# Sending each token's row to its expert slots in DRAM by indirect writes, in place of a one-hot token table and gathers

## The chip, the core and the metric

The kernel runs on one core of one Trainium2 chip. The metric is the device time of one execution in microseconds (us), smaller is better; a comparison takes the median of several runs. One further execution is recorded by the hardware profiler, and every duration below comes from that record.

## What is computed

Cross-attention with a gate, then a mixture of experts with a gate. There are 32 x 128 = 4096 tokens of 256 values, 8 experts, two experts for each token, and room for `cap` = 1024 tokens in each expert. Cut to what matters here:

```python
x = x + tanh(g_xattn) * xattn(layernorm(x), ctx)           # 16 heads of 64
xf = layernorm(x).reshape(4096, 256)
topv, topi = top_k(softmax(xf @ gate_w.T), 2)
gates = topv / topv.sum(-1)
# loc[t, j]: how many tokens chose this expert before this one;
# all first choices count before all second choices
valid = loc < 1024
flat_idx = where(valid, topi * 1024 + loc, 0)
disp = zeros(8 * 1024, 256).at[flat_idx].add(xf * valid)    # dispatch
h = relu(disp_e @ fc1_e.T + fc1_b);  eo = h @ fc2_e + fc2_b # for each expert e
out = (eo[flat_idx] * (gates * valid)).sum(over the two choices)
x = x + tanh(g_ffn) * out
```

## The kernel before, in words

The program has two blocks, one after the other, with a barrier of all five engines between them. Each engine runs a stream of its own that is written out by hand; semaphores order the engines, and no scheduler moves anything. Matrix products with weights are made of three (or five) products of split operands, a high and a low part of each.

**Attention** (`attention`). The tokens go in 8 groups `g` of 512 (`GB` = 4 batches of 128 tokens). A group has 8 steps `j` (`NP`), one for each pair of heads. In a step TensorE computes a queries tile (L591 to L593), a keys tile (L599 to L603), a values tile (L471 to L475), the scores (L514), transposes the probabilities of the step before (L488) and weighs the values of the step before that (L501). VectorE finds the maxima of the scores (L917), normalises (L947), evicts the transposes (L884) and the values (L909). ScalarE takes the exponentials (L722). In step 7 TensorE also transposes the next group's rows (L479, jobs FA and FB), ScalarE writes their high part and VectorE their low part `xT_l` (`low`, L760), which the next group's first query needs. TensorE's results go through two PSUM banks in turn (`take_bank`): a job waits until the job two before it has been evicted.

The routing of group g-1 is spread over the steps of group g: output projection and residual in step 1 (`residual`), second layer norm in step 2 (`normalise`, L779, tile `xn2`), gate logits in step 3 (`route_masks`), ranks in step 4 (`route_counts`), slots in step 5 (`route_slots`), which ends with `hl`, the slot of each token and choice cut into a high and a low part (L865). From `hl` GpSimd and VectorE build one-hot rows (`onehots`, L227, L228, L230). In step 7 TensorE multiplies them in the jobs T0 and T1 (L560), which puts token number and gate at each slot's place, and VectorE adds that to `table` (L936). GpSimd's order in a group is: bias onto the residual rows (L399), two `rstd`, the split of the next context (`split_cv`), the one-hots, then `copy_ck` (L338), whose result `ck` the next group's first keys tile (L599) waits for. SyncE loads x and context of the next group, stores x1 to the output (L285) and the normalised rows to `xn2_dram` (L287). After the last group a tail (`finish`) runs the same routing steps with nothing beside them. `keep_warm` (L111) fills waits of TensorE with products that nobody reads.

**Experts** (`experts`). Each expert has 2 groups `n` of 512 slots, 16 in all. GpSimd gathers the rows of a group from `xn2_dram` by four indirect DMAs (`gather`, L1117), with columns of `index` from the table; TensorE transposes them (`transpose_rows`, L1185), multiplies with fc1 (L1199 to L1201) and fc2 (L1213 to L1215); VectorE adds the bias (L1302), ScalarE scales by the gate (L1258), and GpSimd adds the rows to the output by four indirect DMAs with addition (`scatter`, L1129). GpSimd also makes the low parts of the next expert's weights (L1139, L1141). The transposes of the next group stand in the middle of a group, between fc1 and fc2.

Of the kernel before, what the change touches and what calls it, by code (L numbers as in the profile page):

```python
# [5 lines left out]
P = 128  # L6
# [17 lines left out]
NHI = E * CAP // P  # L24
EH = CAP // P
PAD = 1
# [31 lines left out]
MISC_PREV = {1: ["O0", "O1"], 2: ["XA", "XB"], 3: ["LG"], 4: ["PR"], 7: ["T0", "T1"]}  # L58
# [15 lines left out]
def gated_block(nc, x, ctxT, g_x, g_f, wq, wk, wv, wo, bo, gateT, fc1T, fc1b, fc2, fc2b, out):  # L74
    f32 = mybir.dt.float32

    xn2_dram = nc.dram_tensor("xn2_rows", [N + PAD, D], f32, kind="Internal").ap()
# [3 lines left out]
    xn2_v = xn2_dram[0:N, :].rearrange("(b p) d -> p b d", p=P)  # L81

    with ExitStack() as keep:
# [4 lines left out]
        table = keep.enter_context(nc.sbuf_tensor("table", [P, 2, 2, NHI], f32))  # L88
# [10 lines left out]
        keep2 = keep.enter_context(nc.sbuf_tensor("keep2", [P, E, EH], f32))  # L99
        shared = (keep2, table, running, tanh_g, ident, w1_raw, w2_raw, w1_split, w2_split)  # L100

        with ExitStack() as ctx:
            attention(nc, ctx, sem, x_v, out_v, xn2_v, xn2_dram, ctxT, g_x, g_f, wq, wk, wv, wo, bo, gateT, fc1T, fc2, shared)
        with ExitStack() as ctx:
            experts(nc, ctx, sem, out_rows, xn2_dram, fc1T, fc1b, fc2, fc2b, shared)
# [13 lines left out]
def attention(nc, ctx, sem, x_v, out_v, xn2_v, xn2_dram, ctxT, g_x, g_f, wq, wk, wv, wo, bo, gateT, fc1T, fc2, shared):  # L119
# [7 lines left out]
    keep2, table, running, tanh_g, ident, w1_raw, w2_raw, w1_split, w2_split = shared  # L127
# [19 lines left out]
    onehot_lo = work[:, 1024:2048].rearrange("p (s k) -> p s k", s=8)  # L147
    rows = sb("rows", [P, 4, GB, D])
    xn, xr, x1, xn2 = (rows[:, n] for n in range(4))

    flat_rows = rows.rearrange("p a b d -> p a (b d)")
    wv_raw, wk_raw = [work[:, 0:INNER], flat_rows[:, 1]], [flat_rows[:, 2], flat_rows[:, 3]]
    hi_vals = rows[:, 3].rearrange("p b (two c) -> p (b two) c", two=2)
# [6 lines left out]
    zrow = sb("zrow", [PAD, D])  # L160
# [9 lines left out]
    gates, gdiff, gexp, gden = sb("gates", [P, 2, GB]), sb("gdiff", [P, GB]), sb("gexp", [P, GB]), sb("gden", [P, GB])  # L170
    place, loc, late, slot = sb("place", [P, 2, GB, E]), sb("loc", [P, 2, GB]), sb("late", [P, 2, GB]), sb("slot", [P, 2, GB])
    ranks = sb("ranks", [P, 2 * 2 * GB * E])
    sloti, hl_i = sb("sloti", [P, 2, GB], i32), sb("hl_i", [P, 2, 2, GB], i32)
    hl = sb("hl", [P, 2, 2, GB])
# [4 lines left out]
    def ps(name):  # L179
# [8 lines left out]
        s_consts, s_wo_in, s_c_in, s_x_in, s_xr_in, s_small_in, s_zeros_out, s_w_hi,  # L188
        s_w_lo, s_tanh, s_bias_o, s_zrow, s_q_ready, s_k_ready, s_v_ready, s_s_ready, s_pt_ready,
        s_av_ready, s_o_ready, s_xt_ready, s_lg_ready, s_pr_ready, s_tb_ready, s_f_ready, s_at_hi,  # L190
        s_f_hi, s_q_done, s_k_done, s_v_done, s_pt_done0, s_pt_done1, s_at_split, s_f_split, s_negmax,
        s_exp, s_p_ready, s_o_done, s_xa_done, s_xb_done, s_lg_done, s_pr_done, s_tb_done, s_stats1,
        s_rstd1, s_xn_ready, s_stats2, s_rstd2, s_xn2_ready, s_mask_ready, s_gdiff, s_gexp,
        s_slot_ready, s_onehot0, s_onehot1, s_onehot_last, s_token, s_cv_ready, s_ck_ready, s_xr_ready, s_x1_out, s_xn2_out, s_w_rest,
        s_dve_self, s_pool_self, s_dve_gate, s_pool_gate, s_e0_in, s_c0_hi, s_e0_hi, s_e0_lo,
    ) = (sem("a_" + name) for name in (
        "consts", "wo_in", "c_in", "x_in", "xr_in", "small_in", "zeros_out", "w_hi",
        "w_lo", "tanh", "bias_o", "zrow", "q_ready", "k_ready", "v_ready", "s_ready", "pt_ready",
        "av_ready", "o_ready", "xt_ready", "lg_ready", "pr_ready", "tb_ready", "f_ready", "at_hi",
        "f_hi", "q_done", "k_done", "v_done", "pt_done0", "pt_done1", "at_split", "f_split", "negmax",  # L200
        "exp", "p_ready", "o_done", "xa_done", "xb_done", "lg_done", "pr_done", "tb_done", "stats1",
        "rstd1", "xn_ready", "stats2", "rstd2", "xn2_ready", "mask_ready", "gdiff", "gexp",
        "slot_ready", "onehot0", "onehot1", "onehot_last", "token", "cv_ready", "ck_ready", "xr_ready", "x1_out", "xn2_out", "w_rest",
# [6 lines left out]
    def done(job, g):  # L210

        kind, j = job
        return {
            "Q": (s_q_done, 8 * g + j + 1), "K": (s_k_done, 8 * g + j + 1), "V": (s_v_done, 8 * g + j + V_AHEAD + 1),
            "O0": (s_o_done, 2 * g - 1), "O1": (s_o_done, 2 * g), "XA": (s_xa_done, g), "XB": (s_xb_done, g),
            "LG": (s_lg_done, g), "PR": (s_pr_done, g), "T0": (s_tb_done, 2 * g + 1), "T1": (s_tb_done, 2 * g + 2),
            "FA": (s_f_split, 2 * g + 3), "FB": (s_f_split, 2 * g + 4),
        }[kind]
# [3 lines left out]

    def onehots(engine, j, batches=range(GB)):

        for b in batches:
            n = j * GB + b
            engine.tensor_scalar(onehot_lo[:, n, :], iota[:, :], hl[:, 1, j, b:b + 1], None, ALU.is_equal)  # L227
            engine.tensor_scalar(hi_vals[:, n, 0:NHI], iota[:, 0:NHI], hl[:, 0, j, b:b + 1],  # L228
                                 token[:, b:b + 1], ALU.is_equal, ALU.mult)
            last = engine.tensor_scalar(hi_vals[:, n, NHI:2 * NHI], iota[:, 0:NHI], hl[:, 0, j, b:b + 1],  # L230
                                        gates[:, j, b:b + 1], ALU.is_equal, ALU.mult)
        return last
# [4 lines left out]
    def _(sp):  # L237
# [44 lines left out]
        def store(g, whole):  # L282
# [3 lines left out]
            sp.wait_ge(s_xn2_ready, whole)  # L286
# [1055 lines left out]
```

## Time and profile before

| | us |
|---|---|
| time, median of 3 runs | 1061.38 (1060.06 to 1061.88) |
| the profiled execution: span from first to last instruction | 1058.7 |
| what lies around the span (median less span) | 2.7 |
| attention, 8 groups, to 635 us of the span | 635 |
| tail of the attention and start of the experts | 635 to 680 |
| experts to the end | 680 to 1058.7 |
| TensorE busy | 1015.9 (96%) |
| VectorE, ScalarE, GpSimd busy | 681.8, 478.4, 482.2 |

The profile has a record of one execution alone, and gives its span; its own time outside the span isn't recorded, so the difference to the median of the three runs stands in the table. Busy shares are means over stages with different limits; each stage has to be read by itself.

### The profile page before, as it was taken

What the parts mean: (1) busy time and instruction counts of PE and PEld (TensorE: products, weight loads), DVE (VectorE), ACT (ScalarE), POOL (GpSimd) and SP (SyncE); (2) the same over time, 40 slices, a digit from 0 to 9 for tenths busy, and PEclk for the clock granted to TensorE, in tenths of its full rate; (3) what the DMA queues carried; (4) which work ended last, traced back from release to release, by engine and by line L of the source; (5) the groups of instructions that cost most, each with busy time, mean ns of one, the idle gap of its engine ahead of it and who ended that gap; (6) DMA issues with size and microseconds to landing.
All of it is one profiled execution on the core that took longest, in us unless ns stands there. A gap on an engine that the chain in (4) does not pass through costs nothing. (4 is left out here: it accounts for less than half of the span.)

```text
span 1058.7 us, 21101 instructions
## 1 busy us (share of the span) xinstructions
PE 1015.9 (96%) x7314; PEld 848.5 (80%) x7314; DVE 681.8 (64%) x1605; ACT 478.4 (45%) x1502; POOL 482.2 (46%) x498
## 2 busy tenths in 40 slices
PE   7999999999999999999999988899999999999995
PEld 5678778778778778778778777689999889999885
DVE  5785785785785785885885784455444555544552
ACT  3663453553553553553553551154443535434351
POOL 7521071071071071071080044465858676586756
PEclk9999999999999999999999998999999999999998
DMA  9201110110110120120100101226243361524435
GB/s 241 84 20 42 41 41 20 40 46 13 40 56 3 40 58 1 40 59 1 58 0 11 52 2 40 73 78 144 41 125 62 109 149 37 136 45 110 105 68 66
DMA packets 49948, 63.42 MB, mean 60 GB/s; under 512 B 5976, under 2 KB 41714, under 8 KB 49906
## 3 DMA queue, kind: packets, MB, share of 16 engines
q1 hardware_dynamic: 37234, 45.41, 13.8%
q0 software_dynamic: 12672, 17.47, 9.6%
q8 instruction: 25, 0.41, 0.2%
q14 instruction: 17, 0.14, 0.0%
HBM read 46.45 MB, written 16.78 MB: 60 GB/s over the span
## 5 line engine op out<-in xcount | busy, mean ns | idle before, releaser
L722 ACT ACTIVATE work<-score,negmax 128x128 f32<-128x128 f32 x256 | 90.4, 379 | 88.0 <-DVE negmax L917 88.0
L1250 ACT ACTIVATE hid<-up,b 128x512 f32<-128x512 f32 x128 | 88.2, 689 | 85.6 <-PE up L1201 85.6
L722 ACT ACTIVATE probs_odd<-score,negmax 128x128 f32<-128x128 f32 x256 | 90.4, 381 | 59.9 <-DVE negmax L917 59.9
L1129 POOL DMA_INDIRECT out_dram<-eo,index_e x64 | 106.5, 1664 | 19.5 <-issue 19.2
L343 POOL TENSOR_SCALAR var<-mv 128x4 f32<-128x4 f32 (+1 forms) x17 | 3.8, 225 | 228.8 <-DVE mv L774 222.8
L1302 DVE TENSOR_TENSOR eo_raw<-down,b 128x256 f32<-128x256 f32 x64 | 25.9, 425 | 121.5 <-PE down L1215 121.5
L1295 DVE TENSOR_TENSOR hid_l<-hid,hid_h 128x512 fp32r<-128x512 f32 x128 | 88.7, 693 | 4.4
L514 PE MATMUL score<-k_sb,q_sb 64*128 64x128 f32 x1024 | 87.6, 284 | 1.5 <-issue 1.5
L909 DVE COPY v_sb<-proj 128x512 f32<-128x512 f32 x62 | 42.7, 689 | 71.6 <-PE proj L475 71.5
L675 ACT ACTIVATE q_sb<-proj 128x512 f32<-128x512 f32 x64 | 39.3, 614 | 105.2 <-PE proj L593 104.2
L1293 DVE CAST hid_h<-hid 128x512 fp32r<-128x512 f32 x128 | 54.8, 428 | 47.2 <-ACT hid L1250 45.5
L1258 ACT ACTIVATE eo<-eo_raw,gate_e 128x256 f32<-128x256 f32 x64 | 30.9, 506 | 118.0 <-DVE eo_raw L1302 118.0
L917 DVE TENSOR_REDUCE negmax<-score 128x4 f32<-128x512 f32 x128 | 81.8, 679 | 0.6 <-PE score L514 0.6
L884 DVE COPY pT<-probT 128x512 f32<-128x512 f32 x128 | 81.7, 678 | 0.0
L1117 POOL DMA_INDIRECT rows<-xn_rows,index_e x64 | 68.0, 1063 | 25.1 <-issue 19.7
L514 PEld LDWEIGHTS score<-k_sb,q_sb 64*128 64x128 f32 x1024 | 73.3, 187 | 4.2 <-issue 2.0
L527 PE MATMUL proj<-w_split,aT_h 128*128 128x256 f32 x256 | 73.2, 286 | 0.2 <-DVE aT_l L760 0.2
L528 PE MATMUL proj<-w_split,aT_h 128*128 128x256 f32 x256 | 72.4, 283 | 0.0
L529 PE MATMUL proj<-w_split,aT_l 128*128 128x256 f32 x256 | 72.4, 283 | 0.0
L1213 PE MATMUL down<-w_split,hid_h 128*128 128x256 f32 x256 | 71.5, 279 | 0.0
L1213 PE MATMUL down<-w_h,hid_h 128*128 128x256 f32 x256 | 71.5, 279 | 0.0
L1214 PE MATMUL down<-w_l,hid_h 128*128 128x256 f32 x256 | 70.9, 277 | 0.0
(215 smaller groups left out, 3080.3 us busy)
## 6 DMA issues: line engine op xcount, KB each, us to landing
w_raw<-fc1T_dram SPq DMA_DIRECT2D x9, 1024.0 KB, 5.2
w_raw<-fc_dram SPq DMA_DIRECT2D x9, 1024.0 KB, 9.3
rows<-x_dram SPq DMA_DIRECT2D x16, 512.0 KB, 4.5
out_dram<-rows SPq DMA_DIRECT2D x8, 512.0 KB, 3.0
xn_rows<-rows SPq DMA_DIRECT2D x8, 512.0 KB, 2.9
c_raw<-ctxT_dram SPq DMA_DIRECT2D x8, 256.0 KB, 3.8
c_raw<-ctxT_dram SPq DMA_DIRECT2D x16, 128.0 KB, 4.4
b<-fc2b_dram SPq DMA_DIRECT2D x9, 128.0 KB, 8.5
```

What stands on the lines that cost most here:

```text
L514: last = mm(score[hh][:, t], q_sb[r, t], k_sb[r, t], start=True, stop=True)
L527: mm(o, aT_h[:, j, t], wo_h[:, j, :], start=(j == 0), stop=False)
L528: mm(o, aT_h[:, j, t], wo_l[:, j, :], start=False, stop=False)
L529: last = mm(o, aT_l[:, j, t], wo_h[:, j, :], start=False, stop=(j == NP - 1))
L722: last = nc.scalar.activation(probs[j % 2][:, c, :], score[hh][:, b * P:(b + 1) * P], ACT.Exp, bias=negmax[:, j % 2, c:c + 1], accum_out=s ...
L884: V.tensor_copy(pT[:, j % 2, hh, :], probT[hh][:, :]).then_inc(pt_done, 1)
L917: V.tensor_reduce(negmax[:, j % 2, hh * GB:(hh + 1) * GB], score[hh][:, :].rearrange("p (i k) -> p i k", i=GB), axis=AX, op=ALU.max, negat ...
L1129: pool.indirect_dma_start(out=out_rows[:, :], out_offset=bass.IndirectOffsetOnAxis(ap=index_e[par][:, half * GB + i:half * GB + i + 1], ax ...
L1213: mm(o, hid_h[:, k, t], w2_h[par][:, k, :], start=(k == 0), stop=False)
L1214: mm(o, hid_h[:, k, t], w2_l[par][:, k, :], start=False, stop=False)
L1250: nc.scalar.activation(hid[m % 2][:, :], up[m % 2][:, :], ACT.Relu, bias=b1[par][:, m:m + 1]).then_inc(s_hid, 1)
L1295: V.tensor_tensor(hid_l[:, m, :], hid[m % 2][:, :], hid_h[:, m, :].bitcast(f32), ALU.subtract).then_inc(s_hid_split, 1)
```

## The change

The order of rows in DRAM now is that of the slots. A tensor `disp` of 8192 rows of `W` = 258 values (256 of the normalised token, its number, and its exponential `exp(top2 - top1)`) takes the place of `xn2_dram`. In each group, and once in the tail, GpSimd writes the 512 rows to their two slots by 8 indirect DMAs (`dispatch`), and waits for them at the end of the group (`dispatched`). Slots that no token takes must read as a row of zeros with token number 4096, so SyncE first fills all of `disp` from one `blank` row in each partition, by one DMA. The experts load their rows by plain DMAs of SyncE (`load_rows`), and VectorE reads token number and gate out of the two extra columns (`meta`). One-hots, table, jobs T0 and T1, gathers and the store of `xn2` go. Cut to its core:

```diff
-MISC_PREV = {1: ["O0", "O1"], 2: ["XA", "XB"], 3: ["LG"], 4: ["PR"], 7: ["T0", "T1"]}
+MISC_PREV = {1: ["O0", "O1"], 2: ["XA", "XB"], 3: ["LG"], 4: ["PR"]}
-    xn2_dram = nc.dram_tensor("xn2_rows", [N + PAD, D], f32, kind="Internal").ap()
+    disp = nc.dram_tensor("disp", [E * CAP, W], f32, kind="Internal").ap()
...
 @block.sync (attention)
         sp.dma_start(w2_raw[:, :, :], wo.rearrange("(j p) n -> p j n", p=P)).then_inc(s_wo_in, 16)
-        sp.wait_ge(s_zrow, 1)
-        sp.dma_start(xn2_dram[N:N + PAD, :], zrow[:, :]).then_inc(s_zeros_out, 16)
+        sp.wait_ge(s_blank, 1)
+        sp.dma_start(disp.rearrange("(t p) w -> p t w", p=P),
+                     blank[:, :].unsqueeze(1).to_broadcast([P, E * CAP // P, W])).then_inc(s_blank_out, 16)
...
-            sp.wait_ge(s_xn2_ready, whole)
-            sp.dma_start(xn2_v[:, bass.ds(g * GB, GB), :], xn2).then_inc(s_xn2_out, 16)
...
 @block.gpsimd (attention)
+        def dispatch(g):
+            pool.wait_ge(s_disp_done, g)
+            me.mark(nc.gpsimd.tensor_scalar(token[:, :], token[:, :], float(TOK), None, ALU.add))
+            me.after()
+            copy(packed[:, :, D], token[:, :]).then_inc(s_packed, 1)
+            pool.wait_ge(s_gexp, g)
+            pool.wait_ge(s_slot_ready, g)
+            pool.wait_ge(s_packed, g)
+            for j in range(2):
+                for b in range(GB):
+                    pool.indirect_dma_start(
+                        out=disp[:, :], out_offset=bass.IndirectOffsetOnAxis(ap=slots[:, j, b:b + 1], axis=0),
+                        in_=packed[:, b, :], in_offset=None,
+                        bounds_check=E * CAP - 1, oob_is_err=False).then_inc(s_disp, 16)
+        def dispatched(g):
+            if isinstance(g, int) and g == 0:
+                pool.wait_ge(s_blank_out, 16)
+            else:
+                pool.wait_ge(s_disp, 16 * 2 * GB * g)
+            pool.sem_inc(s_disp_done, 1)
...
-                onehots(nc.gpsimd, 0).then_inc(s_onehot0, 1)
-                if has_next:
-                    onehots(nc.gpsimd, 1, (0, 1, 2)).then_inc(s_onehot1, 1)
...
+                dispatch(g)
             if has_next:
                 pool.wait_ge(s_k_ready, 8 * g + 8)
                 pool.wait_ge(s_cv_ready, g + 2)
                 copy_ck()
+            dispatched(g)
...
 @block.tensor (attention), take_bank
-                pe.wait_ge(s_tb_done, 2 * g - 1 + n)
+                pe.wait_ge(s_f_split, 2 * g + 1 + n)
...
 @block.vector (attention): the gates' three instructions go from route_counts, the slots' rule
 for a second choice needs one step more in route_slots, which ends in
+            dve.wait_ge(s_disp_done, g)
+            V.tensor_tensor(slots[:, :, :], slot[:, :, :], late[:, :, :], ALU.add).then_inc(s_slot_ready, 1)
-                    onehots(V, 1, (0, 1, 2)).then_inc(s_onehot1, 1)
-                onehots(V, 1, (3,)).then_inc(s_onehot_last, 1)
...
 @block.sync (experts)
-            for half in range(2):
-                sp.wait_ge(gathers[half], 16 * GB * (e + 1))
             load_expert(sp, fc1T, fc2, nxt, w1_raw, w2_raw, s_w_in)
...
+            for half in range(2):
+                n = 2 * e + half
+                sp.wait_ge(s_meta, n + 1)
+                load_rows(nxt, half)
+        def load_rows(e, half):
+            src = disp_v[bass.ds(e, 1), half * TOK:(half + 1) * TOK, :]
+            sp.dma_start(rows[half][:, :, :], src.rearrange("o (i p) w -> p (o i) w", p=P)).then_inc(rows_in[half], 16)
+        for half in range(2):
+            load_rows(0, half)
         load_bias(0, 0)
...
 @block.gpsimd (experts): gather, columns and their waits go
 @block.vector (experts), at the start of each group
+        def meta(n, e, half):
+            dve.wait_ge(rows_in[half], 16 * (e + 1))
+            if not (isinstance(e, int) and e == 0):
+                dve.wait_ge(scatters[half], 16 * GB * e)
+                dve.wait_ge(s_eo_ready, GB * n - GB)
+            weight = rows[half][:, :, D + 1]
+            V.tensor_copy(index[half][:, :], rows[half][:, :, D])
+            i = me.mark(V.tensor_scalar(den[:, :], weight, 1.0, None, ALU.add))
+            i = me.mark(V.tensor_tensor(share[:, :], weight, first[...], ALU.max))
+            me.after(i)
+            i = me.mark(V.reciprocal(den[:, :], den[:, :]))
+            me.after(i)
+            V.scalar_tensor_tensor(out=gate[half][:, :], in0=share[:, :], scalar=tanh_g[:, 1:2], in1=den[:, :],
+                                   op0=ALU.mult, op1=ALU.mult).then_inc(s_meta, 1)
```

Three places in the order of the instructions. First TensorE, at the end of a group in the attention loop. Before, from the last transposes of step 7 to the next group's first query:

```order
L488 MATMUL probT<-ident,work 128x128 x3
L501 MATMUL av<-pT,v_sb 64x128 [waits a_pt_done0,a_pt_done1,a_at_split,a_v_done]
L501 MATMUL av<-pT,v_sb 64x128 x7
L560 MATMUL proj<-rows,work 128x128 [waits a_onehot0,a_f_split]
L560 MATMUL proj<-rows,work 128x128 x3
L560 MATMUL proj<-rows,work 128x128 [waits a_onehot_last,a_onehot1,a_f_split]
L560 MATMUL proj<-rows,work 128x128 x3
L591 MATMUL proj<-xT_h,w_split 128x512 [waits a_w_lo,a_f_split,a_tb_done]
```

And with the change (its line numbers are its own):

```order
L486 MATMUL probT<-ident,work 128x128 x3
L499 MATMUL av<-pT,v_sb 64x128 [waits a_pt_done0,a_pt_done1,a_at_split,a_v_done]
L499 MATMUL av<-pT,v_sb 64x128 x7
L580 MATMUL proj<-xT_h,w_split 128x512 [waits a_w_lo,a_f_split]
L581 MATMUL proj<-xT_l,w_split 128x512
```

The eight table products are gone, and the next group's first query follows the weighing of the values; it waits for `xT_l` alone (`a_f_split`).

Second GpSimd, in the same loop, between the split of the next context and the copy of `ck`. Before, 21 one-hot instructions in seven triples stand there:

```order
L361 TENSOR_TENSOR cv_d<-c_raw,c_tmp 128x512 [waits a_pool_self]
L227 TENSOR_SCALAR work<-iota,hl 128x128 [waits a_token,a_slot_ready,a_xn2_out]
L228 TENSOR_SCALAR rows<-iota,hl,token 128x64
L230 TENSOR_SCALAR rows<-iota,hl,gates 128x64
L422 TENSOR_SCALAR token<-token 128x4 [waits a_onehot_last,a_onehot0,a_onehot1]
L338 TENSOR_SCALAR ck_h<-cv_h 128x512 [waits a_k_ready,a_cv_ready]
```

With the change:

```order
L343 TENSOR_TENSOR cv_d<-c_raw,c_tmp 128x512 [waits a_pool_self]
L388 TENSOR_SCALAR token<-token 128x4 [waits a_disp_done]
L320 TENSOR_SCALAR packed<-token 128x4 [waits a_pool_self]
L398 DMA disp<-packed,slots 8192x258 [waits a_packed,a_gexp,a_slot_ready]
L398 DMA disp<-packed,slots 8192x258 x7
L320 TENSOR_SCALAR ck_h<-cv_h 128x512 [waits a_k_ready,a_cv_ready]
L443 REGISTER_ALU [waits a_disp]
```

Eight indirect DMAs take the place of the 21 instructions, ahead of the same copies.

Third SyncE, at the start of the attention, with the change:

```order
L250 DMA w_raw<-wo_dram 128x8x256
L252 DMA disp<-blank 128x64x258 [waits a_blank]
L224 DMA rows<-x_dram 128x4x256 [waits a_f_ready]
L228 DMA c_raw<-ctxT_dram 128x512 [waits a_cv_ready]
```

The fill of 8192 rows stands between the load of the output weights and the load of the second group's x, where before one row of 1 KB was written (L267).

## Rows read from the trace of the kernel before

**Rows 1.** Windows by stage: length, busy us (instructions) per engine, granted clock, DMA share, GB/s

```profile
0.00:635.00 635.00, 612.83 (x4677) 483.99 (x4678) 470.90 (x1166) 310.14 (x1256) 208.37 (x316) 1.00 0.14 42
635.00:680.00 45.00, 36.27 (x203) 31.23 (x203) 19.72 (x77) 4.03 (x7) 21.58 (x20) 0.89 0.14 42
680.00:1059.00 379.00, 366.83 (x2437) 333.30 (x2435) 191.13 (x362) 164.24 (x241) 252.23 (x163) 0.99 0.41 92
```

**Rows 2.** Timeline of TensorE, end of group 2: start, us, what; end of group 7

```profile
233.36 1.09 PE L501 MATMUL av<-pT,v_sb 128*64 128x128 f32 x16
234.38 1.16 PE L560 MATMUL proj<-rows,work 128*128 128x128 f32 x8
236.89 0.47 PE L591 MATMUL proj<-xT_h,w_split 128*128 128x512 f32 x1
238.36 0.40 PE L599 MATMUL proj<-ck_h,wk_h 128*128 128x512 f32 x1
...
628.94 0.66 PE L488 MATMUL probT<-ident,probs_odd 128*128 128x128 f32 x4 [1.20 <-DVE probs_odd L947]
```

**Rows 3.** Timeline of VectorE and GpSimd, the same end of group 2

```profile
222.19 1.05 POOL L227 TENSOR_SCALAR work<-iota,hl 128x128 f32<-128x128 f32 x1 [2.01 <-DVE hl L865]
233.56 1.27 DVE L760 TENSOR_TENSOR xT_l<-proj,xT_h 128x512 fp32r<-128x512 f32 x2
237.45 0.63 POOL L338 TENSOR_SCALAR ck_d<-cv_d 128x512 fp32r<-128x512 f32 x1
```

**Rows 4.** Timeline of the passage from attention to experts

```profile
663.34 0.17 DVE L860 TENSOR_TENSOR sloti<-slot,late 128x8 int32<-128x8 f32 x1
670.34 0.22 DVE L1276 TENSOR_TENSOR index<-table 128x64 uint32<-128x64 f32 x1
671.63 1.31 POOL L1117 DMA_INDIRECT rows<-xn_rows,index  x1 [1.56 <-issue]
681.06 1.00 POOL L1117 DMA_INDIRECT rows<-xn_rows,index  x1 [0.30 <-issue]
670.00 6.17 PE L111 MATMUL down<-w_split 128*128 128x512 f32 x26 [0.65 <-PEq L102]
678.64 1.10 PE L1185 MATMUL rT<-ident,rows 128*128 128x128 f32 x8 [2.46 <-DMA rows<-xn_rows,index]
```

**Rows 5.** TensorE after an idle stretch in the tail: timeline, then windows (granted clock third from the end)

```profile
652.89 1.12 PE L646 MATMUL score<-ident,rows 128*128 128x128 f32 x4 [4.52 <-DVE rows L779]
656.65 2.91 PE L111 MATMUL av<-wk_h 128*128 128x512 f32 x6
...
660.00:661.00 1.00, 1.00 (x5) 0.87 (x5) 0.59 (x4) 0.00 (x0) 0.00 (x0) 0.70 0.00 0
```

**Rows 6.** DMA issues: out<-in, count, KB each, median us to landing

```profile
rows<-x_dram SPq DMA_DIRECT2D x16, 512.0 KB, 4.5
...
w_raw<-wo_dram SPq DMA_DIRECT2D x1, 1024.0 KB, 11.1
...
out_dram<-eo,index_e POOLq DMA_INDIRECT x64, 4.0
...
rows<-xn_rows,index POOLq DMA_INDIRECT x8, 2.8
```

**Rows 7.** Start: SyncE's issues, a window (DMA share, GB/s last), then VectorE and TensorE

```profile
14.12 3.47 SPq L267 DMA_DIRECT2D xn_rows<-zrow  x1
...
23.00:24.00 1.00, 1.00 (x6) 0.55 (x6) 0.00 (x0) 0.13 (x1) 1.00 (x2) 1.00 1.09 352
...
43.20 1.40 DVE L764 BATCH_NORM_STATS2 stats<-rows 128x6 f32<-128x256 f32 x4
50.28 0.69 DVE L947 TENSOR_TENSOR probs_odd<-probs_odd,rsum 128x512 f32<-128x512 f32 x1
...
53.37 1.09 PE L488 MATMUL probT<-ident,probs_odd 128*128 128x128 f32 x8
```

**Rows 8.** GpSimd's last indirect DMA with addition, at the end

```profile
1050.48 1.57 POOL L1129 DMA_INDIRECT out_dram<-eo,index_e  x1 [0.30 <-issue]
```

More of the change, by code:

```diff
@@ L146, in attention @@
     xn2T = work[:, 1024:2048].rearrange("p (k t) -> p k t", k=DK)
[L147 to L149 removed]
+    rows = sb("rows", [P, 3, GB, D])
+    xn, xr, x1 = (rows[:, n] for n in range(3))
+    packed = sb("packed", [P, GB, W])
+    xn2 = packed[:, :, 0:D]
     flat_rows = rows.rearrange("p a b d -> p a (b d)")
[L152 to L153 removed]
+    flat_packed = packed.rearrange("p b w -> p (b w)")
+    wv_raw, wk_raw = [work[:, 0:INNER], flat_rows[:, 1]], [flat_rows[:, 2], flat_packed[:, 0:INNER]]
+    blank = sb("blank", [P, W])
     q_sb, k_sb = sb("q_sb", [P, TOK]), sb("k_sb", [P, TOK])
@@ L443, in _ @@
         start = me.n
-        per = 4
+        per = 5
         with pool.Fori(1, NG - 1) as g:
@@ L553, in misc @@
                 mm(bank[:, 64:128], ones[:, :], flat, start=True, stop=True).then_inc(s_pr_ready, 1)
-            elif kind in ("T0", "T1"):
-                j = int(kind[1])
-                pe.wait_ge((s_onehot0, s_onehot1)[j], g)
-                if j == 1:
-                    pe.wait_ge(s_onehot_last, g)
-                for b in range(GB):
-                    last = mm(bank[:, 0:2 * NHI], onehot_lo[:, j * GB + b, :], hi_vals[:, j * GB + b, :],
-                              start=(b == 0), stop=(b == GB - 1))
-                last.then_inc(s_tb_ready, 1)
             else:
@@ L1040, in experts @@
     b2 = [sb(f"b2_{n}", [P, D]) for n in range(2)]
-    rows = [sb(f"rows_{n}", [P, GB, D]) for n in range(2)]
+    rows = [sb(f"rows_{n}", [P, GB, W]) for n in range(2)]
     rT_h, rT_l = sb("rT_h", [P, DK, TOK], f32r), sb("rT_l", [P, DK, TOK], f32r)
@@ L1046, in experts @@
     eo = [sb(f"eo_{n}", [P, GB, D]) for n in range(2)]
-    NCOL = NHI + EH
-    gate = sb("gate", [P, NHI])
-    index = sb("index", [P, NCOL], u32)
-    index_e = [sb(f"index_e{n}", [P, EH], u32) for n in range(2)]
-    gate_e = [sb(f"gate_e{n}", [P, EH]) for n in range(2)]
+    index = [sb(f"index{n}", [P, GB], u32) for n in range(2)]
+    gate = [sb(f"gate{n}", [P, GB]) for n in range(2)]
+    den, share = sb("den", [P, GB]), sb("share", [P, GB])
     def ps(name):
@@ L1086, in step @@
                 sp.wait_ge(s_w_lo, e)
-            for half in range(2):
-                sp.wait_ge(gathers[half], 16 * GB * (e + 1))
             load_expert(sp, fc1T, fc2, nxt, w1_raw, w2_raw, s_w_in)
@@ L1105, in _ @@
         for half in range(2):
+            sp.wait_ge(rows_in[half], 16 * (E + 1))
             sp.wait_ge(scatters[half], 16 * GB * E)
@@ L1109, in _ @@
     def _(pool):
-        def columns(e, par):
-            nc.gpsimd.tensor_copy(index_e[par][:, :], index[:, bass.ds(e * EH, EH)]).then_inc(s_index_e, 1)
-        def gather(columns_, half):
-            pass_gate(pool, s_pool_gate)
-            for i in range(GB):
-                pool.indirect_dma_start(
-                    out=rows[half][:, i, :], out_offset=None, in_=xn2_dram[:, :],
-                    in_offset=bass.IndirectOffsetOnAxis(ap=columns_[:, half * GB + i:half * GB + i + 1], axis=0),
-                    bounds_check=N + PAD - 1, oob_is_err=False).then_inc(gathers[half], 16)
         def scatter(n, e, par, half):
@@ L1170, in _ @@
                 step(EB * t + i, i)
-        for half in range(2):
-            pool.wait_ge(gathers[half], 16 * GB * (E + 1))
         for done in scatters:
@@ L1178, in _, with transpose_rows @@
         mm = nc.tensor.matmul
-        def transpose_rows(gathered, half):
-            pe.wait_ge(gathers[half], gathered)
+        def transpose_rows(loads, half):
+            pe.wait_ge(rows_in[half], loads)
             for k in range(DK):
@@ L1289, in group @@
                 dve.wait_ge(biases[par], 16 * (e - par) + 32)
-                V.tensor_copy(gate_e[par][:, :], gate[:, bass.ds(e * EH, EH)])
+            meta(n, e, half)
             for m in range(HK):
```

207 lines of the change are left out of this document (67 added, 140 removed).

## The prediction

> **What bounds the kernel now.** First the windows by stage: TensorE is busy for 612.8 of the first 635 us and for 366.8 of the last 379, so in both long stages what counts is what stands in TensorE's own order; between them, from 635 to 680, it is busy for 36.3 of 45 us and its clock was granted at 0.89 [rows 1]. VectorE, ScalarE and GpSimd have room on the average, so their instructions matter only where TensorE waits for one of them. Next, TensorE's timeline at the end of a group: after the weighing (L501) the eight table products (L560) start at 234.38, and the next group's first query (L591) at 236.89 [rows 2]. The same stretch on the other engines shows what will be late next: VectorE ends `xT_l` at 233.56 + 1.27 = 234.83, and GpSimd ends the copy of `ck` at 237.45 + 0.63 = 238.08, just ahead of the keys product at 238.36 [rows 2, 3]. Then the passage to the experts, a chain of small steps with nothing beside it [rows 4], and the start, where SyncE issues its loads one behind the other [rows 7].
>
> **The change, part by part.** The sum is made against the span of 1058.7; the median of the runs is 2.7 above it.
>
> *Table products.* In six of the group ends (groups 1 to 6) 236.89 - 234.38 = 2.51 us of TensorE's order go [rows 2]. The query then waits for `xT_l`, ended at 234.83, 0.45 after 234.38; VectorE has three one-hots less ahead of it, so I give back 0.3: 2.2 each, 6 x 2.2 = **13.2 us saved**; the bounds are 2.51 and 2.06. In group 7 the products are followed by a wait of 1.20 for the normalised probabilities (L947) [rows 2], so taking them out alone would save little there; VectorE however also loses the one-hots and two table additions that stand in front of its maxima and of L947. I estimate **1.5 saved**, between 0.8 and 2.0.
>
> *The writes that take the one-hots' place on GpSimd.* No row shows an indirect write of rows without addition. The nearest by kind is the gather: eight take from 671.63 to 681.06 + 1.00, 10.4 us, 1.3 each [rows 4]. The other bound is the indirect write with addition, 1.57 + 0.30 = 1.87 each, 15.0 for eight [rows 8]. I take the gather: it moves the same rows without arithmetic. GpSimd started its one-hots at 222.19 [rows 3]. A DMA that waits for a VectorE result starts about 1.1 us behind it (index ended at 670.56, DMA at 671.63) [rows 4], so the eight run from about 222.9 to 233.3. Then the copy of `ck`, three times 0.62, ends near 235.2. The keys product comes at 238.36 - 2.2 = 236.2 [rows 2]: the copies are hidden with 1.0 us to spare. **Cost 0**, and the cover is gone once a write takes over (236.2 - 1.9 - 222.9)/8 = 1.43 us. Behind the writes GpSimd waits for their landing; queued behind that wait is the bias on the residual rows of the next group, which is wanted only in step 1. The store of `xn2` that goes was waited for by the one-hots alone.
>
> *The passage to the experts.* The slots are ready about when `sloti` was, 663.34 [rows 4]: three gate instructions less, one dependent step more. The first of eight writes starts 1.1 later, near 664.4, the last near 673.9 (9.43 later), and lands 2.8 behind its issue, as a gather does [rows 6]: 676.7. GpSimd tells SyncE, the barrier opens at about 677.2, where before it opened at 670.0 [rows 4]. SyncE then loads the first 512 rows; such a load lands after 4.5 [rows 6], at 681.7. TensorE meanwhile runs 26 warming products, 6.17 us at full clock [rows 4]. But it has then been idle for some 11 us, since the tail's 24 warming products end near 666. After an idle stretch of 4.52 us the trace shows the clock at half and six such products in 2.91 us, 0.485 each; the window from 660 to 661 has it at 0.70, so it came back at 660.6, 7.7 us after the engine had resumed at 652.89 [rows 5]. I take 6.2 us at half (13 products) and 13 at full speed, 2.7 us together 8.9: the transposes start at 686.1 where they started at 678.64. **7.5 us lost.** Bounds: full clock throughout, 683.4, 4.8 lost; half throughout, 26 x 0.485 = 12.6, 11.2 lost; with writes as dear as those with addition, 5.7 more. VectorE's five small `meta` instructions fit into its wait for the first hidden tile.
>
> *The experts.* TensorE is busy nearly without a gap [rows 1] and nothing in its order changes. GpSimd loses the gathers. At the end the last four writes with addition run back to back up to 1050.48 + 1.57, though the last tile's `eo` was ready some 2 us before, since gathers stood ahead of them; without them the last starts one period earlier, **1.9 us saved** [rows 8].
>
> *The fill.* 8192 rows of 1032 bytes are 8.45 MB, and SyncE's next issue is the second group's x. The queue is already backed up here: the single row of L267 took 3.47 us to issue, and the output weights landed 11.1 us after their issue, at 24.7 [rows 6, 7]. With the engines full the trace moves 352 GB/s [rows 7], so the fill needs at least 24 us. It starts near 23.5; and at most twice that if each row costs as two; I take 27 us, near the lower bound, since its rows are only 8 bytes longer than those of 1024 from which the rate comes, until 50.5. x then moves in 1.5 us and lands near 53.5. VectorE wants it at 43.20 (L764) and its stream waits there [rows 7]: 10.3 us. Queued behind are the eviction of the values, the next maxima and the normalisation for step 3, which ends at 50.28 + 0.69 = 50.97 and is wanted by the transposes at 53.37: 2.4 us of slack [rows 7]. That makes 7.9 lost on TensorE, and about 1.1 more for the half clock after its wait. **9.0 us lost.** Bounds: 0 if x gets past the fill, 33 if each row costs twice.
> The page "DMA: Bandwidth & Descriptors" of the Trainium skill, section "How a descriptor splits into AXI transactions", says that a descriptor which doesn't start at a multiple of 256 bytes fetches from the boundary below. By that rule a 1032-byte row moves about 36 beats of 32 bytes instead of 32, an estimate of 27 us for the fill; the rows of this trace have no such transfer, and the sum is the same by it.
>
> *Sum:* -13.2 - 1.5 - 1.9 + 7.5 + 9.0 = -0.1. Span 1058.6, time **1061.3 us**: no change that can be told. Two gains of the loop and the end are given back at the start and in the passage.
>
> **The rivals.**
>
> *The writes are dear (slower).* If a write takes 1.87 us as those with addition do [rows 8], the eight end at 237.9, the copies of `ck` at 239.8, and the keys product, ready at 236.2, waits 3.6 us: 6 x 3.6 = 22, and 5.7 in the passage. 1061.3 + 27.7 = 1089. It decides from 1.43 us a write. For it: they go to DRAM as those do, and run beside VectorE. Against it: the addition is what they lack.
> The page "DMA: Bandwidth & Descriptors" of the Trainium skill, section "SWDGE vs HWDGE vs iDMA", says that descriptors which GpSimd writes use SBUF state from which VectorE can lock GpSimd out. It speaks against this change, which moves 56 more indirect DMAs beside a busy VectorE; the trace before has no indirect DMA in the attention.
>
> *The fill is slow (slower).* Rows with ragged ends may be written at two thirds of the rate: 36 us, 9 more: 1070.
>
> *The fill holds nobody up (faster).* If x is served beside the fill, or the fill moves at the speed of its first microseconds without the queue before it, the 9.0 go: 1052. Against it stands that SyncE's issue of the x load comes after that of the fill and that issues already block there [rows 7].
>
> **How the numbers follow.** A measurement of this kernel tells about 0.2%, 2.1 us, from no change. The sum as worked: 0.50, by its bounds between 1053 and 1070. Dear writes 0.14, slow fill 0.18, no stall 0.18. The sum's half spreads over both sides of so narrow a band: 0.16 faster, 0.19 within, 0.15 slower. With 0.17 of the case without a stall faster comes to 0.33; within 0.21, which has the rest; slower 0.15 + 0.14 + 0.17 = 0.46. The range has the case without a stall at its low end, 1051, and reaches past the slow fill to 1080; what is left out is most of the dear writes.
>
> **What would show it.** Right: the group ends of the attention 2.2 us shorter from L501 to the next query; eight DMAs per group of 1.0 busy; VectorE's first statistics of the second group waiting for the x load until about 53; the clock at half after the barrier, which opens near 7 us later than before; the last write with addition 2 us sooner behind the last TensorE product. Wrong: a wait of the keys product for `ck` in each group (dear writes); no wait for x at the start; waits of TensorE among the experts for rows or for `meta`, which I cost at nothing.

## The result, and the profile after

The changed kernel takes **1075.08 us** (median of 4 runs, 1073.53 to 1076.21) beside 1060.91 for the kernel before: ratio 1.013, interval 1.012 to 1.014. It is slower by 1.3%, where no change was forecast. The profiled execution spans 1073.7, 15.0 more than before's 1058.7.

The ledger goes by marks that both traces have; each row is the time from the mark above it.

| from the mark above to | before, at | after, at | change | forecast |
|---|---|---|---|---|
| weighing of the values (L501 / L499) in step 2 of group 1 | 112.92 | 127.43 | +14.5 | +9.0 |
| the same of group 7 | 585.49 | 582.82 | -17.2 | -13.2 |
| the slots of the last group | 663.34 | 659.90 | -0.8 | -1.5 |
| the first transposes of the experts | 678.64 | 686.82 | +11.6 | +7.5 |
| start of TensorE's last product | 1047.18 | 1063.98 | +8.6 | 0 |
| the end | 1058.7 | 1073.7 | -1.8 | -1.9 |

Between the first two marks lie six group ends and six output projections.

**The start.** The timelines of SyncE, VectorE and TensorE (start, length, engine and line; in brackets the idle time before and what ended it):

```profile
14.21 3.07 SPq L252 DMA_DIRECT2D disp<-blank  x1
17.33 26.71 SPq L224 DMA_DIRECT2D rows<-x_dram  x1
55.90 1.41 DVE L750 BATCH_NORM_STATS2 stats<-rows 128x6 f32<-128x256 f32 x4 [12.27 <-DMA rows<-x_dram]
58.46 0.80 PE L588 MATMUL proj<-ck_h,wk_h 128*128 128x512 f32 x1 [8.38 <-DVE v_sb L889]
63.08 0.80 PE L469 MATMUL proj<-wv_h,cv_h 128*128 128x512 f32 x1 [1.81 <-ACT q_sb L661]
```

and a window (length, busy us and instructions of PE, PEld, DVE, ACT, POOL, then granted clock, DMA share, GB/s):

```profile
58.00:70.00 12.00, 9.72 (x44) 6.90 (x46) 8.71 (x16) 6.02 (x29) 1.28 (x2) 0.52 0.22 72
```

SyncE's issue of the x load is blocked for 26.7 us behind the fill; VectorE's statistics, at 43.20 before [rows 7], wait until 55.90. TensorE stands for 8.38 + 1.81 = 10.2 us, and runs at 0.52 of its clock for the 12 us after.

**A group's end** (of group 2; TensorE, then GpSimd's last copy of `ck`; the last line is the first write of the kernel, in group 1, and the slowest of all 64):

```profile
244.96 1.09 PE L499 MATMUL av<-pT,v_sb 128*64 128x128 f32 x16
246.01 0.50 PE L580 MATMUL proj<-xT_h,w_split 128*128 128x512 f32 x1
245.93 0.65 POOL L320 TENSOR_SCALAR ck_d<-cv_d 128x512 fp32r<-128x512 f32 x1
158.74 1.67 POOL L398 DMA_INDIRECT disp<-packed,slots  x1 [2.12 <-issue]
```

From the weighing to the next query it is 1.05 us where it was 3.53 [rows 2]: 2.48 saved. A write takes 1.01 on the mean of all 64, so the copies end at 246.58 and no keys product waits for them.

**The passage** (VectorE, GpSimd's first and last write, SyncE, TensorE):

```profile
659.90 0.17 DVE L845 TENSOR_TENSOR slots<-slot,late 128x8 uint32<-128x8 f32 x1
660.95 1.10 POOL L398 DMA_INDIRECT disp<-packed,slots  x1 [10.93 <-DVE slots L845]
...
670.02 0.97 POOL L398 DMA_INDIRECT disp<-packed,slots  x1 [0.30 <-issue]
678.07 0.92 SPq L1052 DMA_DIRECT2D rows<-disp  x2
678.10 8.88 PE L107 MATMUL down<-w_split 128*128 128x512 f32 x26 [15.55 <-PEq L98]
686.82 1.03 PE L1119 MATMUL rT<-ident,rows 128*128 128x128 f32 x8
```

The barrier opens 8.05 us after the last write was issued, where 3.3 had been taken; the 26 warming products take 8.88 (forecast 8.9, 6.17 before [rows 4]). How near that came is partly luck: in other traces of the same 26 products, behind a wait of 10 to 16 us, they take 7.5 to 8.9 us.

**The experts.** TensorE's transposes of two groups in a row, the kernel before, then the changed one:

```profile
738.64 1.03 PE L1185 MATMUL rT<-ident,rows 128*128 128x128 f32 x8
761.40 1.04 PE L1185 MATMUL rT<-ident,rows 128*128 128x128 f32 x8
```

```profile
747.50 1.03 PE L1119 MATMUL rT<-ident,rows 128*128 128x128 f32 x8
770.92 1.04 PE L1119 MATMUL rT<-ident,rows 128*128 128x128 f32 x8
```

A group of 512 rows takes 23.42 us where it took 22.76, with the same products, no idle time of TensorE and the clock at 1.00 in both. The changed kernel has the slow pace in all 15 full groups. The kernel before has the fast one in 13 of them; its first takes 23.39 and its last 23.31. So 13 x 0.65 = 8.5 are lost. Taken apart, the starts of the 256-column products (L1147 to L1149) lie mostly 118.5 ns apart against 113.3, those of the 512-column products 232 against 229.

**The end**: the last write with addition starts at 1066.44, 2.5 us behind TensorE's last product; before it was 3.3 [rows 8].

### The profile page after: what moved, and what is told of

The parts are those of the page before. It is cut to its first block and busy times, and to the rows that moved or that the text cites. A ratio compares the mean times of both kernels' runs of the same rounds, so it can differ in the third digit from the quotient of the medians.

```text
span 1073.7 us, 20682 instructions
## 1 busy us (share of the span) xinstructions
PE 1015.8 (95%) x7186; PEld 845.3 (79%) x7186; DVE 675.9 (63%) x1577; ACT 477.5 (44%) x1502; POOL 377.9 (35%) x345
## 5 line engine op out<-in xcount | busy, mean ns | idle before, releaser
L1081 POOL DMA_INDIRECT out_dram<-eo,index x64 | 102.5, 1602 | 107.3 <-ACT eo L1192 77.0
L398 POOL DMA_INDIRECT disp<-packed,slots x64 | 64.7, 1011 | 72.6 <-DVE slots L845 53.4
L1192 ACT ACTIVATE eo<-eo_raw,gate 128x256 f32<-128x256 f32 x64 | 30.8, 506 | 125.4 <-DVE eo_raw L1244 125.4
L525 PE MATMUL proj<-w_split,aT_h 128*128 128x256 f32 x256 | 72.6, 284 | 0.5 <-DVE aT_l L746 0.5
L1147 PE MATMUL down<-w_h,hid_h 128*128 128x256 f32 x256 | 72.7, 284 | 0.0
L1147 PE MATMUL down<-w_split,hid_h 128*128 128x256 f32 x256 | 72.7, 284 | 0.0
L1149 PE MATMUL down<-w_split,hid_l 128*128 128x256 f32 x256 | 72.1, 282 | 0.0
L1149 PE MATMUL down<-w_h,hid_l 128*128 128x256 f32 x256 | 72.1, 282 | 0.0
L1148 PE MATMUL down<-w_split,hid_h 128*128 128x256 f32 x256 | 72.0, 281 | 0.0
```

The lines of the kernel that those rows point to most:

```text
L398: pool.indirect_dma_start(out=disp[:, :], out_offset=bass.IndirectOffsetOnAxis(ap=slots[:, j, b:b + 1], axis=0), in_=packed[:, b, :], in_o ...
L525: mm(o, aT_h[:, j, t], wo_h[:, j, :], start=(j == 0), stop=False)
L1081: pool.indirect_dma_start(out=out_rows[:, :], out_offset=bass.IndirectOffsetOnAxis(ap=index[half][:, i:i + 1], axis=0), in_=eo[half][:, i, ...
L1147: mm(o, hid_h[:, k, t], w2_h[par][:, k, :], start=(k == 0), stop=False)
L1148: mm(o, hid_h[:, k, t], w2_l[par][:, k, :], start=False, stop=False)
L1149: last = mm(o, hid_l[:, k, t], w2_h[par][:, k, :], start=False, stop=(k == HK - 1))
```

## The experiments

Every set of runs was made on one chip, with the kernel before beside it. In the runs of the result and in two of the five sets that kernel took 1061 (kind A here), in three sets 1067 to 1068 (kind B, "the slower chip" of the expectations). These are two kinds by time and not two chips: the sets of kind A ran on the chips numbered 14 and 2, those of kind B on 1, 7 and 2. Number 2 stands on both sides, so what makes the kinds is open. Comparisons are made within a kind, but not always within a set: `fill_late`, `no_drain` and `shift_after` ran on chip 1, where the kernel before took 1068.2, and the changed kernel of kind B ran on chip 2, where it took 1067.4. Differences of about 1 us between these sets tell nothing.

**Fill behind the loads (kind B).**

```
-sp.wait_ge(s_blank, 1); sp.dma_start(disp..., blank...)
 iteration(0, 1, False)
+sp.wait_ge(s_blank, 1); sp.dma_start(disp..., blank...)
 sp.wait_ge(s_w_lo, 2)
```

> The changed kernel with the fill of disp issued behind the loads of the second group's x and context instead of ahead of them. Theory (the fill delays x, VectorE's stream stalls, TensorE then runs at half clock): the 14.5 us lost between the start and the first group's end go, VectorE's first statistics of the second group start near 43 and not at 55.9, TensorE keeps its full clock from 30 to 70; time about 1060.6. Rival (the fill costs by the bandwidth it takes from other loads, wherever it stands): less than 5 us come back.

Measured 1113.3, beside 1126.3 for the changed kernel on kind B (below): 13.0 less. The absolute time expected, 1060.6, was missed by the waits of kind B, which are told further down. SyncE's and VectorE's timelines, then a window:

```profile
14.23 4.08 SPq L224 DMA_DIRECT2D rows<-x_dram  x1
20.80 0.59 SPq L272 DMA_DIRECT2D disp<-blank  x1
44.64 1.40 DVE L750 BATCH_NORM_STATS2 stats<-rows 128x6 f32<-128x256 f32 x4
```

```profile
40.00:70.00 30.00, 30.00 (x228) 22.46 (x228) 23.75 (x48) 18.05 (x76) 5.74 (x7) 1.00 0.74 202
```

The wait for x is gone and TensorE is busy without a gap at full clock from 40 to 70, while the fill moves beside it. The fill's cost is its place in SyncE's queue, not the bandwidth that it takes from others.

**The barrier without draining (kind B).**

```
-block = ctx.enter_context(nc.Block())
+block = ctx.enter_context(nc.Block(no_gpsimd_drain=True))
```

> The changed kernel with the barrier at the attention's end taken without the draining of GpSimd's DMA rings; every write is still waited for by its semaphore. Theory (the last write has landed at about 672.7, and the 5.3 us from there to the first load at 678.1 are this draining): the barrier opens about 5 us earlier, first load near 673.2, time about 1070. Rival (the writes themselves land that late, 8 us after their issue): the first load stays 8 us behind the last write's start and the time at 1075.

Measured 1122.2, 4.1 less than 1126.3; the 1070 expected was missed by the same waits. GpSimd's last write and SyncE's first load of rows, first in the changed kernel on kind B, then in this one:

```profile
721.95 0.97 POOL L398 DMA_INDIRECT disp<-packed,slots  x1 [0.31 <-issue]
730.00 0.92 SPq L1052 DMA_DIRECT2D rows<-disp  x2
```

```profile
723.84 0.97 POOL L398 DMA_INDIRECT disp<-packed,slots  x1 [0.30 <-issue]
726.85 0.92 SPq L1052 DMA_DIRECT2D rows<-disp  x2
```

8.05 us become 3.01. Landing and barrier are worth 3.0, near the 3.3 forecast; 5.0 was the draining of GpSimd's DMA rings at the end of the block. The kernel before, whose attention has no indirect DMA, shows no such time: there VectorE's last instruction and its first behind the barrier are 0.3 apart. Of the 5.0, 4.5 arrive at the transposes, since the 26 warming products take 8.39 here and 7.81 there.

**Both at once (kind A).**

> The changed kernel with both edits of the first set: the fill behind the loads of the second group, and the barrier without draining GpSimd's rings. Theory (the two costs are apart in time and add up): 14.5 + 5.1 = 19.6 us less than the changed kernel of this set, so 1055 on a chip where that takes 1075. Rival (a part comes back, since the passage waits for something else next, or the clock): under 16 us less.

1054.87 (ratio to before 0.995, interval 0.993 to 0.997) beside 1074.50 in the same set: 19.6 less, the sum expected. By the marks of the ledger 13.6 of it come at the start and 5.6 in the passage. On kind A this already beats the kernel before.

**Place of the operands.** `W` = 258 makes the experts' `rows` 32 bytes longer each, and other tiles ahead went, so `rT`, `hid_h` and `hid_l` lie at 352 over a multiple of 1024 bytes instead of 288. Four runs move them, and nothing of what the engines execute; three more below keep the shift of `placed`:

```
+sb("shift", [P, 16])    # shift_after, shift_before; 168 in aligned0, 240 in placed
 rT_h, rT_l = sb("rT_h", [P, DK, TOK], f32r), sb("rT_l", [P, DK, TOK], f32r)
```

> The changed kernel with 64 bytes of SBUF left free behind the experts' rows, so that rT, hid_h and hid_l lie at 32 instead of 96 bytes over a multiple of 128, as in the kernel before; TensorE's instructions are the same, one for one. Theory (the place of the operands in SBUF sets the pace of the products): a group of 512 rows takes 22.76 us in place of 23.41, 13 to 16 groups of it, time 1066 to 1067. Rival (the pace goes by where the instructions lie): the groups stay at 23.4 and the time at 1075.

> The kernel before with 64 bytes of SBUF left free ahead of the experts' rT, so that rT, hid_h and hid_l lie at 96 instead of 32 bytes over a multiple of 128, as in the changed kernel; nothing else. Theory (place of the operands): groups of 23.4 us in place of 22.76, time about 1069. Rival (place of the instructions): no change, 1061.

> The version with the late fill and without draining, with 960 bytes of SBUF left free ahead of the experts' rT: rT, hid_h and hid_l then lie at the very bytes where the kernel before has them (288 over a multiple of 1024); TensorE's instructions are unchanged. Theory (place of the operands): the groups of the experts take 22.76 us instead of 23.41, 13 of them 8.5 us, time 1046.4 where the version without the shift took 1054.9. Rival (where the instructions lie, or the order around them): 23.41 and 1054.9.

> The same with 672 bytes: rT, hid_h and hid_l at a multiple of 1024. Theory (what counts is a multiple of 128 plus 32, or nearness to a boundary): a pace of its own, 22.76 or better. Rival (only the distance from the weights counts, and any other than that of the kernel before is slow): 23.4. Either shows only what this one place gives.

| run (kind) | base | rT, hid over 1024 | a group takes | time |
|---|---|---|---|---|
| kernel before again (A) | before | 288 | 22.76 (the last: 23.41) | 1060.4 |
| shift_before (B) | before | 352 | 23.42 (two: 23.55) | 1070.7 |
| changed kernel again (A) | after | 352 | 23.41, all | 1074.5 |
| shift_after (B) | after | 416 | 23.38, four of 15: 22.96 | 1124.7 |
| placed (B) | late fill, no draining | 288 | 22.76 in nine of 15, then in turn with 23.38 | 1102.3 |
| aligned0 (B) | late fill, no draining | 0 | 23.43, all | 1108.2 |

> The kernel before unaltered, for its trace on the chip of this set. If the pace of the experts is a matter of where operands lie in SBUF, a group of 512 rows takes 22.76 us here as in the first trace; if it is a matter of the chip, 23.4.

The kernel before, shifted by 64 bytes, has the slow pace in every group, and the changed kernel has the fast one in nine of its 15 groups once these tiles lie where they lay. `placed` and `aligned0` ran in one set, differ in nothing but the size of the shift, and are 5.9 us apart: the place of tiles moves the pace with the instructions unchanged. Transposes of two groups of `placed`:

```profile
755.92 1.03 PE L1120 MATMUL rT<-ident,rows 128*128 128x128 f32 x8
778.68 1.03 PE L1120 MATMUL rT<-ident,rows 128*128 128x128 f32 x8
```

The theory of 32 over a multiple of 128 fell with `shift_after`: it lies so too and has the faster pace in four groups only. Why every second group of `placed` stays at 23.38 is open; the weights lie 1024 bytes lower than before, and `rows` is 32 bytes longer.

The place isn't all of it. The same program at the same places has its first full group at 23.39 us in one trace of the kernel before and at 22.76 in the other; and `placed_clock` (below), which moves no tile of `placed`, has 23.38 there where `placed` has 22.76. Something in the timing counts too, and no run tells what. `shift_before` costs 2.5 us and not the 8 expected. It reaches the transposes only 1.2 us later than the kernel before does on kind A (679.85 and 678.64), so an estimate from these two is that most of the 7 us by which the kernel before is slower on kind B lie in its experts, unshifted. There is no trace of it on kind B, so that is not shown; and `shift_before` alone doesn't prove the effect of the place.

**The clock in the passage, and both.**

```
-wait_warm(24)   # attention's tail      -wait_warm(26)   # ahead of the experts
+wait_warm(68)                           +wait_warm(18)
```

> The version with the late fill and without draining, with 44 more warming products behind the tail's 24 (10.0 us at full speed, in TensorE's wait for the barrier) and 18 instead of 26 behind the barrier. Theory (the 26 products cost 8 us because the clock had fallen, and the rows are there after 4.4): the clock stays at 1.0, the first transposes start about 4.2 us behind the barrier instead of 7.9, time 1051. Rival (the rows land late and the transposes wait for them): under 1.5 us gained.

> Both: the shift of 960 bytes and the kept clock. If the two gains are apart, 1054.9 - 8.5 - 3.5 = 1042.9, 1.7% under the kernel before; if one hides the other, 1046 or more.

> The best version once more: late fill, no draining, the shift of 960 bytes, the kept clock. On a chip where before takes 1061: 1054.9 - 8.5 - 3.5 = 1042.9. On the other 1098.

On kind B kept_clock took 1103.5, in the set of `placed` (1102.3) and `aligned0` (1108.2). The best version, both edits together, took 1098.32 in that set and **1045.19 on kind A** (ratio 0.986, interval 0.984 to 0.987, against before at 1061.41). Within the set the kept clock gives 3.9 on top of the place, and the place 5.2 on top of the kept clock. TensorE's passage in the best version on kind A:

```profile
641.09 16.10 PE L107 MATMUL av<-wk_h 128*128 128x512 f32 x68
657.61 4.35 PE L107 MATMUL down<-w_split 128*128 128x512 f32 x18 [0.41 <-PEq L98]
661.80 1.03 PE L1120 MATMUL rT<-ident,rows 128*128 128x128 f32 x8
```

and that of the version with late fill and no draining:

```profile
658.27 8.10 PE L107 MATMUL down<-w_split 128*128 128x512 f32 x26 [10.49 <-PEq L98]
666.20 1.03 PE L1119 MATMUL rT<-ident,rows 128*128 128x128 f32 x8
```

From the barrier to the transposes it is 4.2 us instead of 7.9; from the slots to the transposes it is 17.6 instead of 21.1, so 3.5 saved, as expected. The place gave 6.2 of the expected 8.5. Together 9.7 of 12.0.

**Fewer writes (kind A).** One of a group's eight; the rows of the other seven are left out.

```
-for j in range(2):                    +for j in range(1):
-    for b in range(GB):               +    for b in range(1):
-pool.wait_ge(s_disp, 16 * 2 * GB * g) +pool.wait_ge(s_disp, 16 * g)
```

> The changed kernel with one of the eight indirect writes of each group, in the passage too; the rows of the other seven are left out. Theory (GpSimd's run of eight writes delays TensorE's signals until it ends): where the changed kernel waits about 6 us in each group of the loop, this one does not, and 40 us go with the waits; beyond that the passage is 7 x 1.28 = 9 us shorter. On a chip where the changed kernel does not wait: only the 9 us, 1066. Rival (the waits have another cause than the writes): 9 us less on either.

> One of the eight indirect writes of each group, the rows of the other seven left out, once more. On the slower chip: if the run of eight writes makes the waits of 6.4 us, they are gone, six of them and what belongs to them, and the time is near 1070; if something else does, it stays above 1110. On the other chip 1063 as before.

1063.17, and 1063.34 in the later set: 11.3 less than the changed kernel, where 9 was expected. The 2.3 between them are what is left of larger differences. From the first write to the transposes the passage is 15.6 us shorter, not 9: 9.1 for seven writes, 4.1 of the draining (the load follows the last write by 3.96 instead of 8.05) and 2.4 of the clock (26 products in 6.16 us instead of 8.59). Each group of the loop is 0.8 longer. VectorE's normalisation of the next group, first in this kernel, then in the changed one:

```profile
241.91 2.25 DVE L765 TENSOR_SCALAR rows<-rows,mv,rstd 128x256 f32<-128x256 f32 x4
```

```profile
240.94 1.38 DVE L765 TENSOR_SCALAR rows<-rows,mv,rstd 128x256 f32<-128x256 f32 x4
```

Without the run of writes GpSimd copies `ck` just then, and VectorE's four instructions take 2.25 instead of 1.38 beside it; beside the issue of writes they lose nothing. The Trainium skill, page "GPSIMD Engine Reference", section "Specifications", says that GpSimd's SBUF interfaces are shared with VectorE and contended for by some VectorE instructions. The rows agree: 2.25 us beside the copies, 1.38 without them.

**Writes in two halves (kind A).** Four writes ahead of the copies of `ck`, four behind.

```
-dispatch(g)                 +dispatch(g, (0,))   # j = 0
 copy_ck()                    copy_ck()
+                            +writes((1,))        # j = 1
```

> The changed kernel with four of a group's writes ahead of the copies of ck and four behind them. On the slower chip: if TensorE's signals are held up for as long as a run of writes lasts, the wait of 6.4 us falls to under 2 and a second one shows up later or not at all; time under 1100. If the number of writes counts and not their place, about 1125. On the other chip within 3 us of the changed kernel.

1079.83 beside 1074.64 for the changed kernel of that set: 5.2 more, and not within 3. Each group is 0.8 longer, by the same collision (the normalisation takes 2.29). What it was made for, kind B, it never saw, so its question stays open.

**The changed kernel itself, four times.**

> The changed kernel unaltered, on the chip of this set, so that the others of the set have it beside them. The four kernels of the first set ran at 1068 (before) and 1111 to 1125 (three variants of the changed kernel) where 1061 and 1075 had been seen. Theory (a difference between chips): here too either 1075 without, or about 1125 with ScalarE's wait of 6 us in each of the six groups of the loop. Rival (the edits of the first set made those waits): 1075 and no such wait, even where before takes 1068.

> The changed kernel unaltered, as the base of this set. 1075 where before takes 1061; where before takes 1068 about 1125, since the three variants of the first set took 1113 to 1125 there.

> The changed kernel unaltered. On the slower chip about 1125: fill_late took 1113 there and should be 14.5 less, no_drain 1122 and should be 5 less. On the other 1075.

1074.5 and 1074.64 on kind A, **1126.30 on kind B** (ratio to before 1.055, interval 1.052 to 1.058). With the runs of the result that makes four. The same change costs 13 to 14 us on one kind and 59 on the other. By the ledger's marks the loop takes 503.0 us instead of 455.4, 7.9 more a group, and from step 2 of group 7 to the slots it is 5.2 more. TensorE's waits and those without a known releaser ("remote") on kind B; the columns are total, times, longest:

```profile
PE proj L469 <- ACT q_sb L661: 34.9, 7, 6.4
...
ACT q_sb L661 <- remote: 36.9, 6, 6.5
POOL ck_h L320 <- remote: 8.5, 5, 1.7
```

On kind A the trace has no "remote" wait. One of them in the timelines of `fill_late`, which has the same (TensorE, GpSimd's last write, ScalarE, GpSimd):

```profile
230.08 0.39 PE L582 MATMUL proj<-xT_h,w_split 128*128 128x512 f32 x1
231.31 0.50 PE L592 MATMUL proj<-ck_d,wk_e 64*128 64x512 f32 x1
...
235.14 0.97 POOL L398 DMA_INDIRECT disp<-packed,slots  x1 [0.30 <-issue]
...
237.63 0.60 ACT L661 ACTIVATE q_sb<-proj 128x512 f32<-128x512 f32 x1 [6.19 <-remote]
...
237.89 0.61 POOL L320 TENSOR_SCALAR ck_h<-cv_h 128x512 fp32r<-128x512 f32 x1 [1.78 <-remote]
```

ScalarE waits for the query product of 230.08 and GpSimd for the keys product of 231.31, both for TensorE alone, and both go on 1.5 to 1.8 us behind the end of the last write, 236.11. The waits are not the changed kernel's alone. `shift_before`, the kernel before on kind B, has four among the experts, each beside GpSimd's indirect DMAs there:

```profile
DVE eo_raw L1303 <- remote: 17.4, 4, 4.4
```

**The best version with few writes (kind B).**

> The best version (late fill, no draining, shift, kept clock) with one of the eight indirect writes of each group; the rows of the other seven are left out. If the run of eight writes makes the waits of 6.4 us on the slower chip, they go: 1098 - 6 x 6.4 - 9 for the passage = 1051 or less. If not, 1089. On the other chip 1045 - 9 + 4 = 1040: the passage is 9 shorter, and each group of the loop 0.7 longer, as in few_writes.

1050.38 beside 1098.32 with all eight, in another set of kind B: 47.9 less, where 6 x 6.4 + 9 = 47.4 was expected. The sum came right by luck. The 9 us of the passage did not come: from the slots to the transposes it is 17.5 us with one write and 17.3 with eight, because the 68 warming products hold the barrier until 663.6 while the one write starts at 651.4. Instead the loop is 42.6 shorter, 7.1 a group and not 6.4, and another 6.3 go ahead of the last slots, where the estimate had no wait. The "remote" waits are gone, and TensorE's for `q_sb` are 2.7 us in all:

```profile
PE proj L469 <- ACT q_sb L661: 2.7, 8, 1.3
```

So the run of writes makes these waits, on kind B. By what path it holds up TensorE's signals, and why not on kind A, no run tells.

## Why the prediction was wrong, step by step

- *Table products, 13.2 saved*: right in kind, small in size. The loop gave 17.2, 2.86 a group. At the products it was 2.48: the give-back of 0.3 for `xT_l` did not come. Another 0.33 a group came in the step ahead (8.52 from weighing to weighing instead of 8.85), which I had not costed. Group 7 gave 0.8 up to the slots instead of 1.5.
- *Writes at 1.3 each, cost 0*: right on kind A, mostly 0.97 to 1.1 and 0.30 between. The rival of dear writes (from 1.43 us each) did not come. The Trainium skill, page "DMA: Bandwidth & Descriptors", section "SWDGE vs HWDGE vs iDMA", says that VectorE can lock GpSimd out of the SBUF state that its descriptors use. No row shows that here: on either kind the kernel's first write took 1.67 us and no other of the 64 more than 1.3. On kind B the writes were as short, and it was others that waited.
- *Passage, 7.5 lost*: 11.6. The writes, their landing and the half clock came near what was worked out (8.88 for 8.9 us); the missing term is the draining at the block's end, 5.0 us. I had charged landing and barrier with 3.3, which is what they take without it.
- *Experts: nothing*: the step that failed outright, 8.6 us. It was priced at nothing because "nothing in its order changes". That was true and not enough: the pace hangs on where tiles lie, and the change moved them. Laying rT and hid back gave 6.2 of the 8.6; the other 2.4, six groups that stay slow, are open.
- *Fill, 9.0 lost*: mechanism right, 14.5 in size. x was there at 55.9 and not at 53.5. By the landings the fill takes at most 31.0 us (53.7, less 22.7 for the output weights), where 27 was estimated. That explains 2.4; the rest is the half clock after the wait, put at 1.1 without a row for it and measured at 14.5 - 10.2 = 4.3 us. The fill that holds nobody up did not come, and the slow one, 36 us, did not either, though 31.0 lies nearly half way to it from 27.
- *End, 1.9 saved*: 1.8.

The errors, +5.5, -4.0, +0.7, +4.1, +8.6 and +0.1, sum to 15.0. The forecast of no change set the gains of the loop and the end against two costs; each cost was short of a part, and a third was not seen. The time lies within the stated range of 1051 to 1080, but that reached so far up for the slow fill, and none of the 8.6 us of the experts was in it: that the range held is luck.

## What to carry to other kernels

A large transfer goes behind the loads that are wanted soon, since its place in the queue costs more than its bytes. When the first indirect DMA enters a block, the block's end gets a draining of GpSimd's rings; where semaphores already cover the landings, it can be left out. When an edit changes the size of a tile, compare the addresses of those behind it, and look at the pace of products whose code is untouched. When a measured sum agrees with the expected one, look whether its terms do: in `best_few` they did not.

## What had not been expected of the hardware

- Products without idle time at the full clock differ by 2.9% in pace (22.76 against 23.41 us a group) with the place of tiles in SBUF. In the output projection it went the other way: the same 256-column products started 121.0 ns apart on the mean before and 118.9 after, in the loop, in every trace. In the tail it was 120.7 before, and after the change 114.3 in one trace and 118.6 in the next of the same program: a part of it isn't the place.
- Where the kernel before differs by 0.6% between two kinds of sets (1061 and 1067 to 1068), the changed kernel differs by 4.8% (1075 and 1126).
- The draining of GpSimd's rings took 5.0 us behind eight indirect writes. Behind a single one, load and write were 3.96 apart against 3.01 without draining.
